# Mixture-of-experts stages on one core: per-tile combination weights from a row in device memory, spread over partitions by DMA, instead of from a selector matmul

## The chip, the core and the metric

The kernel runs on one core of a Trainium2 chip. The metric is the device time of one execution in microseconds, the median of several runs. TensorE (PE) does matmuls into PSUM, VectorE (DVE) and ScalarE (ACT) do elementwise work, GpSimd (POOL) does elementwise work on SBUF alone, SyncE (SP) issues DMAs.

## What is computed

The program is a chain of eight stages on N = 2048 tokens of 128 channels with a layer norm after each. Three of them are mixtures of experts; the change touches only these. For all tokens x, each with a sparse vector of weights `comb` over the experts:

```
m0:  8 experts, top 2:    out = sum_e comb[t,e] * ( gelu(x @ w1[e]) @ w2[e] )
m1: 64 experts, top 6:    out = shared(x) + sum_e comb[t,e] * ( (silu(x @ eg[e].T) * (x @ eu[e].T)) @ ed[e].T )
m2: 160 experts, top 8:   out = shared(x) + sum_e comb[t,e] * ( silu(x @ wg[e].T) @ wd[e].T )
```

Each stage also adds its input. Every expert is computed for every token, and `comb` is zero for those not chosen. A shared expert is one more with the weight 1.

## The kernel before

Activations lie transposed: 128 channels on the partitions, 2048 tokens along them, cut into NQ = 4 quarters of QW = 512. Hidden rows are worked on in units of 128 (one expert of m1 and m2 has 64, so a unit holds two of them; one expert of m0 has 256 and makes two units). m0 has 16 units, m1 33 and m2 81. One unit on one quarter is a tile, so the stages have 64, 132 and 324 tiles, 520 in all.

`Router` scores the experts, chooses and weighs them (`scores`, `weights`, in two halves of the tokens), and scales the chosen weights on ACT (L560). To keep float32 accuracy with bf16 matmuls it then cuts `comb` into three bf16 parts (L563, L565 on ACT, `rest` L651 on DVE), which PE turns (L530) and ACT and DVE copy out into `combT` (L569, L670). `combT` has 126 rows: three parts of a group of GE = 42 experts.

`experts_phase` is one block of five hand-ordered instruction streams, tied by counting semaphores. For tile k of unit s:

- PE: `product` makes the gate sums in three matmuls (fp16 high and low parts, L760); in m1 three more for the up sums; then the selector matmul (L786) multiplies a 126x128 matrix of zeros and ones by `combT` and so puts into a PSUM bank `cb` the 128x512 weights of this tile; then `down` of tile k-3 (three matmuls, L766) adds to the output sums.
- ACT: `h(k) = func(gate sums)` (L809), then `high(k-1)`, the fp16 high part of `hw` (L802).
- DVE: in m1 `hu(k) = h * up sums` (L841); `hw(k) = h (or hu) * cb` (L847); then `low(k-1) = hw - high` as fp16 (L829). Before `hw(k)` (in m1 before `hu(k)`) it waits for `lo_done` of `low(k-2)`, the instruction it issued last, whose input buffer `hw(k)` writes over.
- POOL: per unit, `split` of the next weights in `stage` into fp16 high (L745) and low (L747) parts, when the last `down` that used the slot is done. SP loads `stage` (L726), 128 KB a unit (192 KB in m1).

The banks 0 to 3 hold the output sums, the banks 4 to 7 alternate between gate, up and `cb`. Before gate(k), PE waits for `hw(k-2)`. The loops (`Fori`) have UB units in a body: 4 in m0, 3 in m1 and m2. The selector is reused with every 21 units, so m1 runs two loops one after the other and m2 four (of 7, 7, 7 and 6 bodies); m0 runs one of 4. ACT reloads its activation table (ACT_TABLE_LOAD) at the head of each body of a loop that was entered with another table; a loop that is entered with the right one has no load in it.

## Time and profile before

| | before |
|---|---|
| median of 3 runs | 2400.64 us (2400.48 to 2401.36) |
| profiled execution: its own time | 2406.57 us |
| its span, first to last instruction | 2404.8 us |
| busy: PE / DVE / ACT / POOL | 1962.0 / 1820.5 / 1370.3 / 254.4 us |
| mean granted clock of TensorE | 0.873 of 2.4 GHz |
| m0 / m1 / m2, from first gate to last gate matmul | from 306.8 / 638.2 / 1136.6 us on; the last gate matmul of all starts at 1629.8 us |

The profile was taken in one execution; line numbers are those of the kernel before. A matmul's length in it holds its pipelining (0.38 us for 128x512, while one starts every 0.216 us), so a rate of PE is read from starts or from counts in a window. The idle time of a group has the engine or DMA that ended it behind it.

### The profile page before, as it was taken

Reading aid. Unit: us, or ns where it says so; the run is one execution under the profiler, and the core shown is the slowest. Engines: PE = TensorE matmul, PEld = TensorE weight load, DVE = VectorE, ACT = ScalarE, POOL = GpSimd, SP = SyncE. Lnnn points to the kernel's source line nnn. Section 1 sums busy time; section 2 is a strip of 40 time slices with the busy share of each in tenths; the row PEclk is TensorE's granted clock in tenths of the full one; section 3 lists DMA queues with packets and bytes.
Section 4 is the critical chain, followed back from the end, with each engine's and each line's share of the span. In section 5 each row is a group of like instructions: output and inputs, shape, how many; then the busy total and the mean of one; then the engine's idle time right before and its main releaser. Section 6 shows DMA issues by size and latency. Waiting matters only on the chain. (4 is left out here: it accounts for less than half of the span.)

```text
span 2404.8 us, 49561 instructions
## 1 busy us (share of the span) xinstructions
PE 1962.0 (82%) x17365; PEld 1230.6 (51%) x17365; DVE 1820.5 (76%) x4154; ACT 1370.3 (57%) x3474; POOL 254.4 (11%) x321
## 2 busy tenths in 40 slices
PE   6999798576699996674999999996777676774987
PEld 5999644454344443453444444444455354443775
DVE  4444578787699996786888888887777877886776
ACT  5666477234455554644777777775455554553555
POOL 1000111000122221000222222220000000000000
PEclk9999899788699998896999999997878787785785
DMA  2000000100100000000000000000000000000000
GB/s 72 4 4 4 26 18 2 37 1 0 36 23 23 23 16 14 1 1 25 22 20 22 22 22 22 22 15 15 13 0 13 13 0 13 13 0 28 2 1 18
DMA packets 32343, 37.82 MB, mean 16 GB/s; under 512 B 4858, under 2 KB 30074, under 8 KB 31956
## 3 DMA queue, kind: packets, MB, share of 16 engines
q1 hardware_dynamic: 32212, 36.04, 5.1%
q8 instruction: 87, 1.43, 0.2%
q14 instruction: 44, 0.36, 0.0%
HBM read 33.40 MB, written 1.05 MB: 14 GB/s over the span
## 5 line engine op out<-in xcount | busy, mean ns | idle before, releaser
L809 ACT ACTIVATE m_h<-ps 128x512 f32<-128x512 f32 x520 | 310.4, 597 | 281.1 <-PE ps L760 280.9
L829 DVE TENSOR_TENSOR m_hwlo<-m_hw,m_hwhi 128x512 f16<-128x512 f32 x523 | 365.7, 699 | 0.3
L847 DVE TENSOR_TENSOR m_hw<-m_h,ps 128x512 f32<-128x512 f32 x388 | 267.0, 688 | 93.1 <-ACT m_h L809 81.1
L802 ACT ACTIVATE m_hwhi<-m_hw 128x512 f16<-128x512 f32 x523 | 325.4, 622 | 1.5 <-DVE m_hw L847 1.5
L760 PE MATMUL ps<-x_hi,m_whi 128*128 128x512 f16 x652 | 248.6, 381 | 4.6 <-issue 4.4
L760 PE MATMUL ps<-x_lo,m_whi 128*128 128x512 f16 x652 | 248.8, 382 | 0.0
L760 PE MATMUL ps<-x_hi,m_wlo 128*128 128x512 f16 x652 | 248.8, 382 | 0.0
L766 PE MATMUL ps<-m_hwhi,m_whi 128*128 128x512 f16 x529 | 201.6, 381 | 1.7 <-DVE m_hwlo L829 1.7
L766 PE MATMUL ps<-m_hwhi,m_wlo 128*128 128x512 f16 x529 | 200.6, 379 | 0.0
L766 PE MATMUL ps<-m_hwlo,m_whi 128*128 128x512 f16 x529 | 200.3, 379 | 0.0
L786 PE MATMUL ps<-m_combT,m_sel 126*128 126x512 bf16 x520 | 199.3, 383 | 0.0
L459 DVE TENSOR_TENSOR rn_s_lo<-rn_s_full,rn_s_hi 128x32 f16<-128x32 f32 x512 | 98.8, 193 | 131.1 <-ACT rn_s_full L416 131.1
L361 PE MATMUL ps<-rn_s_hi,rn_weights 128*128 128x8 f16 x4080 | 186.7, 169 | 0.0
L95 PE MATMUL ps<-ident,ln_x 128*128 128x128 f32 x320 | 75.0, 424 | 96.3 <-DVE ln_x L123 96.3
L414 ACT ACTIVATE rn_s_hi<-ps 128x32 f16<-128x32 f32 x512 | 100.9, 197 | 87.4 <-PE ps L378 47.4
L361 PEld LDWEIGHTS ps<-rn_s_hi,rn_weights 128*128 128x128 f16 x4080 | 149.1, 105 | 0.0
L378 PE MATMUL ps<-rn_s_lo,rn_weights 128*128 128x8 f16 x2040 | 141.1, 175 | 0.0
L747 POOL TENSOR_TENSOR m_wlo<-m_stage,m_whi 128x256 f16<-128x256 f32 (+1 forms) x130 | 134.9, 1038 | 10.4
L745 POOL CAST m_whi<-m_stage 128x256 f16<-128x256 f32 (+1 forms) x130 | 55.2, 425 | 722.1 <-PE ps L766 713.2
L95 PEld LDWEIGHTS ps<-ident,ln_x 128*128 128x128 f32 x320 | 63.3, 222 | 106.1 <-DVE ln_x L123 105.2
L841 DVE TENSOR_TENSOR m_hu<-m_h,ps 128x512 f32<-128x512 f32 x132 | 90.8, 688 | 24.9 <-PE ps L760 15.4
L760 PEld LDWEIGHTS ps<-x_hi,m_whi 128*128 128x128 f16 x652 | 63.0, 97 | 87.8 <-DVE m_hw L847 8.0
(435 smaller groups left out, 4614.5 us busy)
## 6 DMA issues: line engine op xcount, KB each, us to landing
m_stage<-in_m_w SPq DMA_DIRECT2D x97, 128.0 KB, 2.0
m_stage<-in_m_w SPq DMA_DIRECT2D x33, 192.0 KB, 2.3
lj_w<-in_lj_w SPq DMA_DIRECT2D x6, 768.0 KB, 4.3
lq_w<-in_lq_w SPq DMA_DIRECT2D x1, 1536.0 KB, 6.1
m_sel<-in_c_sel_pairs SPq DMA_DIRECT2D x2, 661.5 KB
la_w<-in_la_w SPq DMA_DIRECT2D x1, 1280.0 KB, 5.4
rn_rows<-in_L_attn_rows SPq DMA_DIRECT2D x4, 256.0 KB, 4.3
rn_xs<-rn_xn_hi SPq DMA_DIRECT2D x32, 32.0 KB, 1.9
```

The source lines that it names most:

```text
L95: last = nc.tensor.transpose(ps[:, G + g, j * P:(j + 1) * P], rows[:, 4 * g + j, :], ident[:])
L361: nc.tensor.matmul(sums[:, c, :], wt[:, n, :], s_hi[:, prev, n * B:(n + 1) * B], start=False, stop=False, skip_group_check=True)
L378: last = nc.tensor.matmul(sums[:, c, :], at_hi[:, n, :], s_lo[:, prev, n * B:(n + 1) * B], start=False, stop=(c == GP - 1), skip_group_che ...
L414: nc.scalar.activation(s_hi[:, t % (2 * K), g * W:(g + 1) * W], slot(g, t), ACT.Tanh)\
L747: nc.gpsimd.tensor_tensor(w_lo[:, s, :], stage[:, s, :], w_hi[:, s, :], ALU.subtract)\
L760: last = nc.tensor.matmul(out, a[:, s, cols], b[:, cut], start=(a is w_hi and b is x_hi), stop=(a is w_lo))
L766: last = nc.tensor.matmul(acc[n], a[:, s, COLS - P:COLS], b[:, k4, :], start=False, stop=False, skip_group_check=True)
L786: nc.tensor.matmul(cb, sel[0:3 * GE, bass.ds(j * UB + s, 1), :].rearrange("p u m -> p (u m)"), combT[0:3 * GE, g, n * QW:(n + 1) * QW], st ...
L802: nc.scalar.activation(hw_hi[:, k % 4, :], hw[:, k % 2, :], ACT.Copy).then_inc(hi_done, 1)
L809: nc.scalar.activation(h[:, k % 2, :], ps[:, 4 + (3 * k % 4 if gated else k % 2), :], func)\
L829: nc.vector.tensor_tensor(hw_lo[:, k % 4, :], hw[:, k % 2, :], hw_hi[:, k % 4, :], ALU.subtract)\
L847: nc.vector.tensor_tensor(hw[:, k % 2, :], src[:, k % 2, :], cb, ALU.mult).then_inc(hw_done, 1)
```

## The change

The selector matrices, `combT` in bf16 parts, and the cutting into parts are gone, and with them GE, the groups and the split of m1's and m2's loops: each stage is one loop now (4, 11 and 27 bodies).

The router turns the float32 weights directly (four transposes of 128x128 to a PSUM bank: a "turn" of 512 tokens and up to 128 experts; 4 turns in m0 and m1, 8 in m2), DVE and ACT copy out every other one, and ACT issues for each a DMA that stores it in a device-memory tensor with one row of 2048 float32 for each expert (m0_shares, m1_shares, m2_shares; 8, 66 and 162 rows).

In the expert loop, SP loads after the weights of a unit, and once all rows are stored, two DMAs into `comb`, a float32 tile of 128 x UB x 2048: each reads one row of 8 KB 64 times and writes it to 64 partitions, 512 KB each. They wait until the `hw` of the unit UB before is done. DVE waits once a unit for both and then takes the second operand of `hw` from SBUF. The selector matmul and its PSUM banks are gone, so the gate sums of m0 and m2 have four banks: PE may run gate(k) when `h(k-4)` is done (m1: `h(k-2)`), no longer after `hw(k-2)`. POOL's loop is the same but for the merged loops.

```diff
-        self.NG = NG = combT.shape[1]
-        self.EX = NG * GE
+        self.chunks = [slice(c, min(c + P, EX)) for c in range(0, EX, P)]
+        self.turns = [(h, c, q) for h in range(2) for c in range(len(self.chunks)) for q in range(2)]
...
-        self.comb, self.parts = sb("comb", [P, NT, self.EX]), sb("parts", [P, NT, NG, 3, GE], BF16)
+        self.comb, self.combT = sb("comb", [P, NT, EX]), sb("combT", [P, len(self.chunks), N])
...
+    def turned(self, n):
+        h, c, q = self.turns[n]
+        rows = self.chunks[c].stop - self.chunks[c].start
+        at = (2 * h + q) * QW
+        return self.combT[0:rows, c, at:at + QW], self.S.psum[0:rows, 4 + n % 4, :], self.rows[self.chunks[c], at:at + QW]
...
+        for n, (h, c, q) in enumerate(self.turns):
+            cols = self.chunks[c]
+            pe.wait_ge(self.scaled, h + 1)
+            if n >= 4:
+                pe.wait_ge(self.comb_out[n % 2], (n - 4) // 2 + 1)
+            for j in range(4):
+                last = nc.tensor.transpose(ps[0:cols.stop - cols.start, 4 + n % 4, j * P:(j + 1) * P],
+                                           self.comb[:, 8 * h + 4 * q + j, cols], self.S.ident[:])
+            last.then_inc(self.comb_up, 1)
         for engine in range(2):
-            pe.wait_ge(self.comb_out[engine], self.NG)
+            pe.wait_ge(self.comb_out[engine], len(self.turns) // 2)
...
-            act.wait_ge(self.scaled, h + 1)
-            nc.scalar.activation(self.parts[:, halves[h], :, 0, :], self.comb_v(h), ACT.Copy).then_inc(self.part0, 1)
-            act.wait_ge(self.rest1, h + 1)
-            nc.scalar.activation(self.parts[:, halves[h], :, 1, :], self.comb_v(h), ACT.Copy).then_inc(self.part1, 1)
-        for n in range(1, 2 * self.NG, 2):
-            act.wait_ge(self.comb_up, n + 1)
-            half, g = n // self.NG, n % self.NG
-            nc.scalar.activation(self.combT[0:3 * GE, g, half * 1024:(half + 1) * 1024],
-                                 ps[:, 4 + n % 4, :].bitcast(BF16)[0:3 * GE, :], ACT.Copy).then_inc(self.comb_out[1], 1)
+        for n in range(len(self.turns)):
+            out, turned, rows = self.turned(n)
+            if n % 2:
+                act.wait_ge(self.comb_up, n + 1)
+                nc.scalar.activation(out, turned, ACT.Copy).then_inc(self.comb_out[1], 1)
+            act.wait_ge(self.comb_out[n % 2], n // 2 + 1)
+            act.dma_start(rows, out).then_inc(self.stored, 16)
...
-        def rest(h, part):
-
-            dve.wait_ge(self.part0 if part == 0 else self.part1, h + 1)
-            out = self.comb_v(h) if part == 0 else self.parts[:, self.halves[h], :, 2, :]
-            nc.vector.tensor_tensor(out, self.comb_v(h), self.parts[:, self.halves[h], :, part, :], ALU.subtract)\
-                .then_inc(self.rest1 if part == 0 else self.part2, 1)
...
-        rest(0, 0)
-        rest(0, 1)
-        rest(1, 0)
-        turned(0, self.NG)
-        rest(1, 1)
-        turned(self.NG, 2 * self.NG)
-
-
-def experts_phase(nc, S, ctx, tag, weights, selector, combT, func, gated, UB, route):
+        for n in range(0, len(self.turns), 2):
+            out, turned, _ = self.turned(n)
+            dve.wait_ge(self.comb_up, n + 1)
+            nc.vector.tensor_copy(out, turned).then_inc(self.comb_out[0], 1)
...
+    assert bodies * UB == U
+    AHEAD = 2 if gated else 4
     LAG = 3
...
+    comb_got = [S.sems.new(f"{tag}_comb_got{s}") for s in range(UB)]
...
-    sel = sb("sel", [P, NSEL, P], BF16)
+    comb = sb("comb", [P, UB, N], F32)
...
+    def gate_bank(k):
+        return ps[:, 4 + (2 * (k % 2) if gated else k % 4), :]
+
+    def up_bank(k):
+        return ps[:, 5 + 2 * (k % 2), :]
...
-            sp.dma_start(sel[0:3 * GE], selector).then_inc(sel_got, 16)
-            for u0, bodies, _ in runs:
-                with sp.Fori(0, bodies) as j:
-                    for s in range(UB):
-                        sp.wait_ge(split_done, j * UB + (u0 + s + 1))
-                        sp.dma_start(stage[:, s, :], weights[bass.ds(j * UB + (u0 + s), 1)]
-                                     .rearrange("u p c -> p (u c)")).then_inc(slot_got[s], 16)
+            with sp.Fori(0, bodies) as j:
+                for s in range(UB):
+                    sp.wait_ge(split_done, j * UB + (s + 1))
+                    sp.dma_start(stage[:, s, :], weights[bass.ds(j * UB + s, 1)]
+                                 .rearrange("u p c -> p (u c)")).then_inc(slot_got[s], 16)
+                    if s == 0:
+                        sp.wait_ge(route.stored, 16 * len(route.turns))
+                    sp.wait_ge(hw_done, j * (4 * UB) + (4 * s + 4))
+                    for half in range(2):
+                        row = bass.ds(2 * (j * UB + s) + half, 1) if halves else bass.ds(j * (UB // 2) + s // 2, 1)
+                        sp.dma_start(comb[half * 64:half * 64 + 64, s, :], route.rows[row].broadcast_to([64, N]))\
+                            .then_inc(comb_got[s], 16)
...
-            for u0, bodies, g in runs:
-                with pe.Fori(0, bodies) as j:
-                    for s in range(UB):
-                        pe.wait_ge(split_done, j * UB + (u0 + s + 1 + UB))
-                        for n in range(NQ):
-                            k = 4 * s + n
-                            kk = j * (4 * UB) + (4 * u0 + k)
-                            R = 3 * k if gated else None
-                            hb = ps[:, 4 + (R % 4 if gated else k % 2), :]
-                            cb = ps[:, 4 + ((R + 2) % 4 if gated else 2 + k % 2), :]
-                            pe.wait_ge(hw_done, kk + 1)
-                            product(hb, slice(0, P), s, n).then_inc(gate_done, 1)
-                            if gated:
-                                pe.wait_ge(act_done, kk + 1)
-                                product(ps[:, 4 + (R + 1) % 4, :], slice(P, 2 * P), s, n).then_inc(up_done, 1)
-                                pe.wait_ge(hu_done, kk + 1)
-                            nc.tensor.matmul(cb, sel[0:3 * GE, bass.ds(j * UB + s, 1), :].rearrange("p u m -> p (u m)"),
-                                             combT[0:3 * GE, g, n * QW:(n + 1) * QW], start=True, stop=True)\
-                                .then_inc(comb_done, 1)
-                            pe.wait_ge(lo_done, kk + 1)
-                            down((s if n >= LAG else s - 1) % UB, (n - LAG) % NQ, (k - LAG) % 4)
+            with pe.Fori(0, bodies) as j:
+                for s in range(UB):
+                    pe.wait_ge(split_done, j * UB + (s + 1 + UB))
+                    for n in range(NQ):
+                        k = 4 * s + n
+                        kk = j * (4 * UB) + k
+                        pe.wait_ge(act_done, kk + (5 - AHEAD))
+                        product(gate_bank(k), slice(0, P), s, n).then_inc(gate_done, 1)
+                        if gated:
+                            pe.wait_ge(hu_done, kk + 1)
+                            product(up_bank(k), slice(P, 2 * P), s, n).then_inc(up_done, 1)
+                        pe.wait_ge(lo_done, kk + 1)
+                        down((s if n >= LAG else s - 1) % UB, (n - LAG) % NQ, (k - LAG) % 4)
...
-            act.sem_inc(act_done, 1)
+            act.sem_inc(act_done, 4)
...
-            for u0, bodies, _ in runs:
-                with act.Fori(0, bodies) as j:
-                    for k in range(4 * UB):
-                        kk = j * (4 * UB) + (4 * u0 + k)
-                        act.wait_ge(gate_done, kk + 1)
-                        nc.scalar.activation(h[:, k % 2, :], ps[:, 4 + (3 * k % 4 if gated else k % 2), :], func)\
-                            .then_inc(act_done, 1)
-                        act.wait_ge(hw_done, kk + 2)
-                        high(k - 1)
-            act.wait_ge(hw_done, 4 * U + 2)
+            with act.Fori(0, bodies) as j:
+                for k in range(4 * UB):
+                    kk = j * (4 * UB) + k
+                    act.wait_ge(gate_done, kk + 1)
+                    nc.scalar.activation(h[:, k % 2, :], gate_bank(k), func).then_inc(act_done, 1)
+                    act.wait_ge(hw_done, kk + 4 * UB)
+                    high(k - 1)
...
-            dve.sem_inc(hw_done, 2)
+            dve.sem_inc(hw_done, 4 * UB)
             dve.sem_inc(lo_done, LAG - 1)
             if gated:
-                dve.sem_inc(hu_done, 1)
+                dve.sem_inc(hu_done, 2)
...
+            with dve.Fori(0, bodies) as j:
+                for s in range(UB):
+                    for n in range(NQ):
+                        k = 4 * s + n
+                        kk = j * (4 * UB) + k
                         src = h
-                        dve.wait_ge(act_done, kk + 2)
+                        dve.wait_ge(act_done, kk + 5)
                         dve.wait_ge(lo_done, kk + 2)
                         if gated:
                             dve.wait_ge(up_done, kk + 1)
-                            nc.vector.tensor_tensor(hu[:, k % 2, :], h[:, k % 2, :], ps[:, 4 + (3 * k + 1) % 4, :],
-                                                    ALU.mult).then_inc(hu_done, 1)
+                            nc.vector.tensor_tensor(hu[:, k % 2, :], h[:, k % 2, :], up_bank(k), ALU.mult).then_inc(hu_done, 1)
                             src = hu
-                            dve.wait_ge(hu_done, kk + 2)
-                        dve.wait_ge(comb_done, kk + 1)
-                        cb = ps[:, 4 + ((3 * k + 2) % 4 if gated else 2 + k % 2), :]
-                        nc.vector.tensor_tensor(hw[:, k % 2, :], src[:, k % 2, :], cb, ALU.mult).then_inc(hw_done, 1)
+                            dve.wait_ge(hu_done, kk + 3)
+                        if n == 0:
+                            dve.wait_ge(comb_got[s], j * 32 + 32)
+                        nc.vector.tensor_tensor(hw[:, k % 2, :], src[:, k % 2, :], comb[:, s, n * QW:(n + 1) * QW], ALU.mult)\
+                            .then_inc(hw_done, 1)
                         dve.wait_ge(hi_done, kk + 1)
                         low(k - 1)
...
-    moe(nc, S, "m0", 8, A["m0_w"], A["c_sel_halves"], ACT.Gelu, False, 4,
+    moe(nc, S, "m0", 8, A["m0_w"], A["m0_shares"], False, ACT.Gelu, False, 4,
```

## Rows read from the trace of the kernel before

**Rows 1.** Groups by line of the page: busy, mean ns, idle before and releaser

```profile
L786 PE MATMUL ps<-m_combT,m_sel 126*128 126x512 bf16 x520 | 199.3, 383 | 0.0
```

**Rows 2.** Windows, one body each, last ten bodies: busy (instructions) by engine, PEclk, DMA

```profile
358.31:382.76 24.45, 24.42 (x114) 10.81 (x113) 21.00 (x33) 19.05 (x33) 5.40 (x8) 1.00 0.04 11
...
769.97:795.92 25.95, 25.95 (x122) 11.68 (x121) 23.76 (x37) 14.66 (x25) 5.41 (x7) 1.00 0.08 23
...
1249.34:1267.70 18.36, 18.33 (x86) 8.05 (x85) 15.77 (x25) 14.57 (x25) 4.00 (x6) 1.00 0.08 21
1267.70:1449.40 181.70, 181.70 (x841) 81.60 (x840) 156.73 (x241) 133.75 (x241) 41.76 (x60) 1.00 0.07 22
```

**Rows 3.** Timeline around a loop boundary in m2: start us, length, engine, line

```profile
1175.16 0.62 ACT L802 ACTIVATE m_hwhi<-m_hw 128x512 f16<-128x512 f32 x1
1175.30 0.69 DVE L847 TENSOR_TENSOR m_hw<-m_h,ps 128x512 f32<-128x512 f32 x1 [0.17 <-ACT m_h L809]
1175.80 1.28 ACT L809 ACT_TABLE_LOAD   x1
...
1177.10 0.60 ACT L809 ACTIVATE m_h<-ps 128x512 f32<-128x512 f32 x1
...
1177.82 0.69 DVE L847 TENSOR_TENSOR m_hw<-m_h,ps 128x512 f32<-128x512 f32 x1 [1.23 <-ACT m_h L809]
...
1178.42 0.68 DVE L829 TENSOR_TENSOR m_hwlo<-m_hw,m_hwhi 128x512 f16<-128x512 f32 x1
...
1179.19 0.69 DVE L847 TENSOR_TENSOR m_hw<-m_h,ps 128x512 f32<-128x512 f32 x1
...
1180.92 0.67 POOL L747 TENSOR_TENSOR m_wlo<-m_stage,m_whi 128x256 f16<-128x256 f32 x1
...
1181.18 0.96 DVE L829 TENSOR_TENSOR m_hwlo<-m_hw,m_hwhi 128x512 f16<-128x512 f32 x1
```

**Rows 4.** Timeline of another split of weights in m2

```profile
1149.80 0.40 POOL L745 CAST m_whi<-m_stage 128x256 f16<-128x256 f32 x1 [4.65 <-PE ps L766]
...
1149.95 0.80 DVE L829 TENSOR_TENSOR m_hwlo<-m_hw,m_hwhi 128x512 f16<-128x512 f32 x1
...
1150.28 0.99 POOL L747 TENSOR_TENSOR m_wlo<-m_stage,m_whi 128x256 f16<-128x256 f32 x1
...
1150.86 0.69 DVE L847 TENSOR_TENSOR m_hw<-m_h,ps 128x512 f32<-128x512 f32 x1
```

**Rows 5.** Timeline of VectorE in m1

```profile
804.24 0.69 DVE L841 TENSOR_TENSOR m_hu<-m_h,ps 128x512 f32<-128x512 f32 x1
804.97 0.69 DVE L847 TENSOR_TENSOR m_hw<-m_hu,ps 128x512 f32<-128x512 f32 x1
...
806.35 0.69 DVE L841 TENSOR_TENSOR m_hu<-m_h,ps 128x512 f32<-128x512 f32 x1
```

**Rows 6.** ACT groups by line and form: ACT table loads

```profile
L809 ACT ACT_TABLE_LOAD x18 | 23.1, 1283 | 0.3
```

**Rows 7.** Window in the stage before m2: busy by engine, granted clock (1.00)

```profile
1000.00:1020.00 20.00, 17.59 (x203) 12.94 (x201) 18.56 (x45) 11.01 (x23) 0.00 (x0) 1.00 0.01 2
```

**Rows 8.** Timeline at the end of m2's router

```profile
1120.02 0.20 DVE L645 RECIPROCAL m2r_rec<-m2r_sum 128x8 f32<-128x8 f32 x1
...
1122.91 2.64 ACT L560 ACTIVATE m2r_comb<-m2r_comb,m2r_rec 128x160 f32<-128x160 f32 x8
...
1138.85 0.69 DVE L847 TENSOR_TENSOR m_hw<-m_h,ps 128x512 f32<-128x512 f32 x1 [3.80 <-ACT m_h L809]
```

**Rows 9.** Windows in which the DMA queues were full: last columns share, GB/s

```profile
8.00:10.00 2.00, 0.73 (x4) 0.33 (x2) 0.00 (x0) 1.98 (x12) 0.00 (x0) 1.00 1.02 268
2185.00:2186.00 1.00, 0.00 (x0) 0.00 (x0) 0.00 (x0) 0.00 (x0) 0.00 (x0) 0.50 1.13 467
```

**Rows 10.** DMA issues of the page: KB each, us to landing

```profile
m_stage<-in_m_w SPq DMA_DIRECT2D x97, 128.0 KB, 2.0
```

**Rows 11.** SP's timeline: length of one DMA issue

```profile
2181.41 0.43 SPq L1856 DMA_DIRECT2D lq_w<-in_lq_w  x1
```

More of the change, by code:

```diff
@@ L663, in vector, with experts_phase @@
         weights(1)
-        def turned(first, last):
-            for n in range(first, last):
-                if n % 2 == 0:
-                    dve.wait_ge(self.comb_up, n + 1)
-                    half, g = n // self.NG, n % self.NG
-                    nc.vector.tensor_copy(self.combT[0:3 * GE, g, half * 1024:(half + 1) * 1024],
-                                          ps[:, 4 + n % 4, :].bitcast(BF16)[0:3 * GE, :]).then_inc(self.comb_out[0], 1)
-        rest(0, 0)
-        rest(0, 1)
-        rest(1, 0)
-        turned(0, self.NG)
-        rest(1, 1)
-        turned(self.NG, 2 * self.NG)
-def experts_phase(nc, S, ctx, tag, weights, selector, combT, func, gated, UB, route):
+        for n in range(0, len(self.turns), 2):
+            out, turned, _ = self.turned(n)
+            dve.wait_ge(self.comb_up, n + 1)
+            nc.vector.tensor_copy(out, turned).then_inc(self.comb_out[0], 1)
+def experts_phase(nc, S, ctx, tag, weights, halves, func, gated, UB, route):
     U, _, COLS = weights.shape
-    NSEL = selector.shape[1]
+    bodies = U // UB
+    assert bodies * UB == U
+    AHEAD = 2 if gated else 4
     LAG = 3
@@ L689, in experts_phase @@
     acc = [ps[:, n, :] for n in range(NQ)]
[L690 to L692 removed]
+    zeroed = S.sems.new(f"{tag}_zeroed")
+    gate_done, up_done, act_done, hu_done, hw_done, hi_done, lo_done, down_done, split_hi, split_done, \
+        split_start = S.sems.new(*(f"{tag}_{n}" for n in ("gate", "up", "act", "hu", "hw", "hi", "lo", "down",
                                                           "split_hi", "split", "split_start")))
     slot_got = [S.sems.new(f"{tag}_slot{s}") for s in range(UB)]
+    comb_got = [S.sems.new(f"{tag}_comb_got{s}") for s in range(UB)]
     x_hi, x_lo = S.x_hi, S.x_lo
@@ L709, in open_sums @@
                              skip_group_check=True)
-    runs = []
-    for g in range((U + NSEL - 1) // NSEL):
-        runs.append((g * NSEL, (min(U, (g + 1) * NSEL) - g * NSEL) // UB, g))
-    assert sum(r[1] for r in runs) * UB == U
+    def gate_bank(k):
+        return ps[:, 4 + (2 * (k % 2) if gated else k % 4), :]
+    def up_bank(k):
+        return ps[:, 5 + 2 * (k % 2), :]
     with nc.Block(no_gpsimd_drain=True) as block:
@@ L830, in low @@
                     .then_inc(lo_done, 1)
-            for u0, bodies, _ in runs:
-                with dve.Fori(0, bodies) as j:
-                    for k in range(4 * UB):
-                        kk = j * (4 * UB) + (4 * u0 + k)
+            with dve.Fori(0, bodies) as j:
+                for s in range(UB):
+                    for n in range(NQ):
+                        k = 4 * s + n
+                        kk = j * (4 * UB) + k
                         src = h
-                        dve.wait_ge(act_done, kk + 2)
+                        dve.wait_ge(act_done, kk + 5)
                         dve.wait_ge(lo_done, kk + 2)
@@ L2227 @@
         A[name] = nc.dram_tensor(f"in_{name}", a.shape, mybir.dt.from_np(a.dtype), kind="ExternalInput").ap()
+    for name, rows in (("m0_shares", 8), ("m1_shares", 66), ("m2_shares", 162)):
+        A[name] = nc.dram_tensor(name, (rows, N), F32).ap()
     out = nc.dram_tensor("out", (B, T, C), F32, kind="ExternalOutput").ap()
```

71 lines of the change are left out of this document (22 added, 49 removed).

## Prediction, made before the changed kernel was run

> **What bounds the kernel now.** I read the groups by line first. The selector matmul is a group of 520 with 0.0 us of idle before it [rows 1]: PE runs it back to back with its neighbours, so it costs PE time wherever PE sets the pace. Then the windows, one loop body each, tell where that is. Ten bodies of m2 take 181.70 us and hold 841 matmuls, which is 120 tiles of 7 [rows 2]: 0.216 us a matmul, 1.514 us a tile, PE never idle, granted clock 1.00. Likewise m1: 122 records, 12 tiles of 10 matmuls, 25.95 us, 2.163 us a tile. So all three stages are bound by PE, and a tile would be 6 x 0.216 = 1.30 us of PE (m0, m2) or 9 x 0.216 = 1.95 us (m1) without the selector.
>
> The next limit is DVE, and busy shares hide how near it is. In m2 its two instructions follow each other at 0.60 us (hw to low, 1177.82 to 1178.42), and at 0.77 us (low to the next hw, 1178.42 to 1179.19) [rows 3]: the second step is the whole length of `low`, 0.68, and 0.09 until the semaphore lets `hw` go, since `hw(k)` waits for the `low` just issued. That wait is in the changed code too. A tile can't be under 0.60 + 0.77 = 1.37 us on DVE. In m1, `hu` to `hu` is 2.11 us with no idle between [rows 5]; its floor is 2.11, just 0.05 below PE's 2.163.
>
> **The change, part by part.**
>
> *Selector matmul removed.* It takes 0.216 us of PE from each of 520 tiles, 112 us in all. But the pace goes over to DVE at once: the floor falls from 1.514 to 1.37 (not 1.30) in m0 and m2, and from 2.163 to 2.11 (not 1.95) in m1. For a body: m2 12 x 1.37 = 16.44 us, m0 16 x 1.37 = 21.92, m1 12 x 2.11 = 25.32. The gate banks, now four, keep PE ahead: its wait is for a `down` behind `low`, and from there to the `hw` four tiles on, there is room. ACT does two instructions of 0.60 and 0.62 a tile and isn't near 1.37. PE will have gaps of some 0.1 to 0.2 us a tile. A stage with PE at 17.59 of 20 us kept the clock at 1.00 [rows 7], so I give the clock nothing.
>
> *`hw` reads its weights from SBUF, not PSUM.* This is the term that decides. POOL splits each unit's weights in two instructions, and in the trace these and `low`, which reads two SBUF tiles, shut each other out. `low`, issued 0.15 us after the cast at 1149.80, takes 0.80 instead of 0.68, so the cast held it until 0.27 after its start; the subtraction issued at 1150.28 takes 0.99 instead of its 0.67 alone, so it began at 1150.60, which is 0.53 after `low` really began (1150.07) [rows 3, 4]. And `low` issued 0.26 after a subtraction that ran at once takes 0.96, so that one held for 0.54 [rows 3]. `hw` with one input in PSUM is not touched: 0.69 in the middle of a subtraction [rows 4]. After the change `hw` has the operands of `low`, so I count it as `low`. In m2 the split is released by a `down` that follows `low(j)`: 0.68 for `low`, 0.05, two matmul starts 0.43, and some 0.60 to POOL makes 1.76 us after the start of `low(j)`. `low(j+1)` then reads (1.37 to 1.90), the cast gets in from 1.90 to 2.17, and `hw(j+3)`, due at 2.14, is 0.03 late. The subtraction asks at about 2.38, when `hw(j+3)` reads until 2.70, and holds until 3.24; `low(j+2)`, due 0.60 after `hw`, at 2.77, is 0.47 late. Sum c = 0.50 us a unit. If DVE kept its turn from `hw` to `low` (due only 0.07 us after `hw` lets go), the subtraction would slip in after `low` and delay `hw` by 0.30: c = 0.33. I take 0.50, since the release at 0.53 comes before the next issue at 0.60. The ends are 0 and 0.50 + 0.20. In m1 the same walk lets the cast in behind `hw` and delays `low` by 0.33, and puts the subtraction beside `hu`, which has a PSUM input: c = 0.33, ends 0 and 0.80.
>
> The Trainium skill (SBUF — State Buffer, "Who interferes with whom") says the same of any VectorE instruction with two SBUF inputs against a GpSimd one that reads SBUF: whoever issues first keeps the port for its whole instruction. It speaks for counting `hw` like `low`; no row here shows an `hw` of this form.
>
> *One loop for each stage.* ACT loads its table 18 times at L809 [rows 6]: 4 in m0, 7 in m1's first loop, 7 in m2's first, none in the later loops. With single loops these are 4, 11 and 27. Before, a load costs m2's body 18.36 - 18.17 = 0.19 us [rows 2]. Paced by DVE it costs more: from `high` (1175.16) over the load and `h` to `hw` (1177.82) is 2.66 us [rows 3], `high` starts 0.69 + 0.03 after its `hw`, so from one `hw` to the second after it is 3.38 against 2 x 1.37 = 2.74: 0.64 us a body. Ends 0.19 and 0.70. In m1 the same path ends at 3.3 against 3.5 for DVE, so the load stays hidden.
>
> *The bodies.* m2: 16.44 + 3 x 0.50 + 0.64 = 18.58, times 27 = 501.7; before 7 x 18.36 + 20 x 18.17 = 491.9 [rows 2]: **+9.8 us**. m0: 21.92 + 4 x 0.50 + 0.64 = 24.56 against 24.45, four bodies: +0.4. m1: 25.32 + 3 x 0.33 = 26.31 against 25.95, eleven bodies: +4.0.
>
> *Router.* Gone: two conversions on ACT and two subtractions on DVE for each half, and bf16 transposes. New: float32 transposes, copies, stores, a wait for the stores, and 1 MB that must land before the first `hw`. In m2, weighing of half two ends on DVE at 1120.2; the scaling takes 2.64 us [rows 8], to 1122.9. ACT then has 4 copies of 0.60 and 8 issues of 0.43 [rows 11], which makes 5.8, to 1128.7, the last store 2.0 us to land [rows 10], two issues 0.9, 2 us fixed and 1.05 MB at 268 GB/s [rows 9] 3.9 us: 1137.5, against 1138.85 for the first `hw` before [rows 8]. So -1.3 for m2; with fewer removed steps about +2 in m0 and 0 in m1. Together +0.3; ends -8 and +12 by the rate of the DMAs. ACT's issues have the whole loop's `h` behind them, but that waits for this data anyway.
>
> *1 MB a unit by DMA.* Per unit 1.05 MB and 0.13 MB of weights. m2's unit is 18.58 / 3 = 6.2 us, so 190 GB/s are enough to hide it; the queues ran at 268 and 467 GB/s in full windows, with rows of 4 KB and 12 KB to 128 partitions [rows 9]. SP's three issues, 1.3 us a unit [rows 11], fit. Behind SP's new wait for the `hw` of unit u-3 stands the weights' load of the next unit, used more than a unit later, and the rows for unit u have two units of time. I take it as hidden. No row shows a DMA to 64 partitions of this size or one that reads the same 8 KB 64 times; the nearest rows give 2.5 to 4.4 us a unit, and if half the partitions gave half the rate, 5.1 to 8.8.
>
> The Trainium skill speaks against this part (SBUF — State Buffer, "Door 1: The DMA port swizzle"): partitions 0 to 63 reach 8 of 16 ports, 196 GB/s measured for 1 MiB and about 218 at best, and two DMAs to the two halves go one after the other. By it the rows would take 4.8 to 5.4 us and the weights 0.3, an estimate from that page: 5.1 to 5.7 us a unit, hidden under my 6.2, but not under m2's floor without POOL, 5.7.
>
> *Sum:* +9.8 + 0.4 + 4.0 + 0.3 = +14.5 us. The profiled execution took 2406.57 us (span 2404.8), so it would show 2421.1; the runs' median lies 5.9 below it, and the same sum on it is 2400.6 + 14.5 = **2415**. This case reaches from 2396 (c = 0.33 in m2 and m0, a load at 0.4) to 2430.
>
> **The rivals.**
>
> *B: the new `hw` doesn't collide with POOL, or little (faster).* For it: only `low` was seen to. Against: same operands. With c = 0: m2's body 17.08, 27 x 17.08 = 461.2, -30.7; m0 22.56, -7.6; m1 25.32, -6.9; the start +0.3: 2355.7. With half the collisions about 2385.
>
> *C: the row DMAs set the pace (far slower).* One mechanism: two half-width transfers in a row, all from one 8 KB row. It decides from 1.18 MB / 6.2 us = 190 GB/s downwards; it makes m2 slower than before from 1.18 / 6.06 = 195. For it: half of 268 is 134. Against: half of 467 is 233. At 170 GB/s a unit of m0 and m2 takes 6.94 us, (6.94 - 6.07) x 97 units = +84: about 2490 with the slower starts; at 134, 8.8 us and 2690. Its sign would be DVE waiting for `comb` at the first tile of each unit.
>
> *D: PE stays the bound* (1.30 us a tile, 324 x 0.214 = 69 us gained in m2 alone). I exclude it: `low` and its semaphore alone stand against it, unless `low` to `hw` gets shorter.
>
> **How the numbers follow.** Forecast 0.58, B 0.24, C 0.18. Range: leaving out B's lowest tenth and C below 175 GB/s or so leaves 2356 to 2470. What a measurement here can tell from no change is about 0.2%, 4.8 us. Faster: B and 0.03 of the forecast's low end, 0.27. Same: 0.11 of the forecast and 0.01 of C, 0.12. Slower: 0.44 and 0.17, 0.61.
>
> **What would show it.** In m2 after: `low` to `hw` at 0.77 and tiles at 1.37 away from splits; `hw` or `low` of 1.0 to 1.2 us beside each POOL subtraction; bodies near 18.6 (m0 24.6, m1 26.3); 27 table loads with a DVE idle of 0.6 behind each; no idle of DVE that a DMA of `comb` ends, but for the first of each stage. It is wrong if `hw` keeps 0.69 beside POOL (B), if `comb` ends idle time at each unit (C), or if the clock falls below 1.00 in the loops.

## The result and the profile after

The kernel after takes 2414.11 us, the median of 12 runs (2404.91 to 2419.51), beside 2401.02 for the kernel before in 12 runs (2397.67 to 2404.4): ratio 1.0052, 95% interval 1.004 to 1.0064, so 9.6 to 15.4 us slower. The forecast was 2415, which is 14.5 us above the kernel before. The profiled execution took 2408.58 us (span 2406.8).

That one lies only 2 us above the profiled execution of before, which would mislead. The start of the layer norm ahead of m0 and that of the one behind m2 tell more. View: ACT's timeline, first before, then after (start us, length, engine, line):

```profile
271.19 0.30 ACT L151 ACTIVATE ln_sd<-ln_mv,epsilons 128x8 f32<-128x8 f32 x1 [1.82 <-DVE ln_mv L110]
...
1639.80 0.30 ACT L151 ACTIVATE ln_sd<-ln_mv,epsilons 128x8 f32<-128x8 f32 x1 [2.34 <-DVE ln_mv L110]
...
1911.16 0.30 ACT L151 ACTIVATE ln_sd<-ln_mv,epsilons 128x8 f32<-128x8 f32 x1 [7.83 <-DVE ln_mv L110]
1955.81 0.30 ACT L151 ACTIVATE ln_sd<-ln_mv,epsilons 128x8 f32<-128x8 f32 x1 [1.82 <-DVE ln_mv L110]
```

```profile
270.24 0.30 ACT L151 ACTIVATE ln_sd<-ln_mv,epsilons 128x8 f32<-128x8 f32 x1 [1.82 <-DVE ln_mv L110]
...
1648.50 0.30 ACT L151 ACTIVATE ln_sd<-ln_mv,epsilons 128x8 f32<-128x8 f32 x1 [1.82 <-DVE ln_mv L110]
...
1919.56 0.30 ACT L151 ACTIVATE ln_sd<-ln_mv,epsilons 128x8 f32<-128x8 f32 x1 [7.65 <-DVE ln_mv L110]
1960.83 0.30 ACT L151 ACTIVATE ln_sd<-ln_mv,epsilons 128x8 f32<-128x8 f32 x1 [1.82 <-DVE ln_mv L110]
```

From first to second it is 1368.61 us before and 1378.26 after: the three expert stages and the unchanged layers between them cost **9.65 us** more. Behind m2 the code is the same, yet one layer there took 44.65 us before (1911.16 to 1955.81) and 41.27 after. Such steps of some 3 us fall differently in other profiled executions too (from the layer norm behind m2 to the end it is 754 to 765 us in all the traces, whatever the edit); they can hide a difference of this size in one pair of executions.

The groups by line and form, and the DMA issues, of after:

```profile
L806 DVE TENSOR_TENSOR m_hwlo<-m_hw,m_hwhi 128x512 f16<-128x512 f32 x523 | 409.7, 783 | 0.3
L824 DVE TENSOR_TENSOR m_hw<-m_h,m_comb 128x512 f32<-128x512 f32 x388 | 273.5, 705 | 69.1 <-DMA m_comb<-m_shares 25.0 <-ACT m_h L787 12.5
L753 PE MATMUL ps<-m_hwhi,m_whi 128*128 128x512 f16 x529 | 208.6, 394 | 72.6 <-DVE m_hwlo L806 66.8
L787 ACT ACT_TABLE_LOAD x42 | 53.9, 1283 | 2.4 <-ACT m1r_combT L564 0.6 <-ACT m0r_combT L564 0.6 <-ACT m2r_combT L564 0.5
...
m_comb<-m_shares SPq DMA_DIRECT2D x260, 512.0 KB, 6.3
m_stage<-in_m_w SPq DMA_DIRECT2D x97, 128.0 KB, 5.9
```

The selector group [rows 1] is gone, and PE now waits for DVE: 66.8 us before `down`, ended by `low` (L753). `low` was 0.699 on the mean before and is 0.783; table loads went from 18 [rows 6] to 42; the weights land 5.9 us behind their issue, 2.0 before [rows 10]. The 25.0 us that the row DMAs end are 10.4 in m0 and 14.6 in m2, each at the first `hw` of its stage. The `hw` of m1 form a group of their own, with 5.7 us at the first.

Windows of one body in m1 and in m2, and of three bodies, of after (length; busy PE, PEld, DVE, ACT, POOL with instructions; granted clock, DMA share, GB/s):

```profile
723.88:750.22 26.34, 25.32 (x110) 9.59 (x109) 24.71 (x36) 14.68 (x25) 6.03 (x6) 1.00 0.61 142
...
1202.60:1220.93 18.33, 16.96 (x74) 6.06 (x73) 17.04 (x24) 15.61 (x26) 4.58 (x6) 1.00 0.86 193
...
1300.00:1355.00 55.00, 50.90 (x218) 18.15 (x216) 51.11 (x73) 46.84 (x76) 13.76 (x18) 1.00 0.87 194
```

m2's body takes 18.33 us with 12 matmuls fewer, against 18.17 and 18.36 [rows 2]. PE, whose rows filled 181.70 of 181.70 us there, has gaps now. The timelines of ACT, DVE and POOL at the head of such a body show what keeps DVE from its 1.37 us a tile. The first line is the `low` beside the last split of the body before:

```profile
1309.74 1.15 DVE L806 TENSOR_TENSOR m_hwlo<-m_hw,m_hwhi 128x512 f16<-128x512 f32 x1
...
1310.49 1.28 ACT L787 ACT_TABLE_LOAD   x1
...
1310.99 0.69 DVE L824 TENSOR_TENSOR m_hw<-m_h,m_comb 128x512 f32<-128x512 f32 x1
...
1312.60 0.69 DVE L824 TENSOR_TENSOR m_hw<-m_h,m_comb 128x512 f32<-128x512 f32 x1 [0.31 <-ACT m_h L787]
1313.21 0.68 DVE L806 TENSOR_TENSOR m_hwlo<-m_hw,m_hwhi 128x512 f16<-128x512 f32 x1
1313.93 0.69 DVE L824 TENSOR_TENSOR m_hw<-m_h,m_comb 128x512 f32<-128x512 f32 x1
1314.54 0.69 DVE L806 TENSOR_TENSOR m_hwlo<-m_hw,m_hwhi 128x512 f16<-128x512 f32 x1
...
1314.97 0.51 POOL L733 CAST m_whi<-m_stage 128x256 f16<-128x256 f32 x1 [4.63 <-PE ps L753]
1315.56 0.99 POOL L735 TENSOR_TENSOR m_wlo<-m_stage,m_whi 128x256 f16<-128x256 f32 x1
...
1315.26 0.77 DVE L824 TENSOR_TENSOR m_hw<-m_h,m_comb 128x512 f32<-128x512 f32 x1
1315.95 1.16 DVE L806 TENSOR_TENSOR m_hwlo<-m_hw,m_hwhi 128x512 f16<-128x512 f32 x1
1317.21 0.69 DVE L824 TENSOR_TENSOR m_hw<-m_h,m_comb 128x512 f32<-128x512 f32 x1
```

Away from splits the pace is near what was foreseen: `low` to `hw` is 0.72 here (1313.21 to 1313.93) and 0.79 most often in m2, `hw` to `low` 0.61 (1313.93 to 1314.54), so a tile takes 1.33 to 1.40. `hw` beside the cast takes 0.77, `low` beside the subtraction 1.16. All over m2, 77 `low` take 1.15 or 1.16 us: about one a unit.

### The profile page after: what moved, and what is told of

It reads as the page before. It is cut to its first block and busy times, and to the rows that moved or that the text cites. A ratio compares the mean times of both kernels' runs of the same rounds, so it can differ in the third digit from the quotient of the medians.

```text
span 2406.8 us, 49587 instructions
## 1 busy us (share of the span) xinstructions
PE 1910.8 (79%) x16797; PEld 1135.3 (47%) x16797; DVE 1859.8 (77%) x4142; ACT 1419.0 (59%) x3487; POOL 277.9 (12%) x321
## 3 DMA queue, kind: packets, MB, share of 16 engines
q8 instruction: 83, 1.36, 0.2%
## 5 line engine op out<-in xcount | busy, mean ns | idle before, releaser
L806 DVE TENSOR_TENSOR m_hwlo<-m_hw,m_hwhi 128x512 f16<-128x512 f32 x523 | 409.7, 783 | 0.3
L824 DVE TENSOR_TENSOR m_hw<-m_h,m_comb 128x512 f32<-128x512 f32 x388 | 273.5, 705 | 69.1 <-DMA m_comb<-m_shares 25.0
L753 PE MATMUL ps<-m_hwhi,m_whi 128*128 128x512 f16 x529 | 208.6, 394 | 72.6 <-DVE m_hwlo L806 66.8
L753 PE MATMUL ps<-m_hwlo,m_whi 128*128 128x512 f16 x529 | 202.8, 383 | 0.0
L753 PE MATMUL ps<-m_hwhi,m_wlo 128*128 128x512 f16 x529 | 202.5, 383 | 0.0
L753 PEld LDWEIGHTS ps<-m_hwhi,m_whi 128*128 128x128 f16 x529 | 51.1, 97 | 305.2 <-DVE m_hwlo L806 302.0
L733 POOL CAST m_whi<-m_stage 128x256 f16<-128x256 f32 (+1 forms) x130 | 77.9, 599 | 708.0 <-PE ps L753 548.1
L735 POOL TENSOR_TENSOR m_wlo<-m_stage,m_whi 128x256 f16<-128x256 f32 (+1 forms) x130 | 135.5, 1042 | 10.4
L747 PEld LDWEIGHTS ps<-x_hi,m_whi 128*128 128x128 f16 x652 | 64.2, 99 | 89.1 <-issue 10.4
L1954 ACT ACTIVATE lq_e<-ps,lq_neg 128x256 f32<-128x256 f32 x128 | 59.6, 470 | 77.9 <-DVE lq_neg L2017 58.6
```

Source lines behind the costliest of these rows:

```text
L735: nc.gpsimd.tensor_tensor(w_lo[:, s, :], stage[:, s, :], w_hi[:, s, :], ALU.subtract)\
L747: last = nc.tensor.matmul(out, a[:, s, cols], b[:, cut], start=(a is w_hi and b is x_hi), stop=(a is w_lo))
L753: last = nc.tensor.matmul(acc[n], a[:, s, COLS - P:COLS], b[:, k4, :], start=False, stop=False, skip_group_check=True)
L806: nc.vector.tensor_tensor(hw_lo[:, k % 4, :], hw[:, k % 2, :], hw_hi[:, k % 4, :], ALU.subtract)\
L824: nc.vector.tensor_tensor(hw[:, k % 2, :], src[:, k % 2, :], comb[:, s, n * QW:(n + 1) * QW], ALU.mult)\
```

## The experiments

All edits are to the kernel after, but for two that are to the kernel before. A time without a number of runs beside it is that of one execution. The diffs show the lines that matter, and `...` stands for the rest.

**POOL's splits of later bodies taken out.**

```diff
-            with pool.Fori(0, bodies) as j:
-                ... split of unit j * UB + s
+            for s in range(UB):
+                ... split of unit s
+            with pool.Fori(0, bodies - 1) as j:
+                ... the same waits, and pool.sem_inc(split_done, 1), for each unit
```

> The kernel after, but POOL splits the weights of the first body of each expert stage only; every later unit uses the split weights of the first body again (they are loaded as before, not used), so the output is another. SP's loads, the row transfers, and all work of PE, ACT and DVE stay. Theory (DVE sets the pace, and each low of about 1.15 us, where 0.68 is the rule, is POOL's subtraction beside it): no low or hw above 0.8 us, m2's unit falls from 6.1 to about 5.6, its body from 18.33 to about 17.1, m1's low from 0.99 to 0.69 and its body from 26.35 to some 25.5 to 26.0, the whole about 2414 - 27 x 1.2 - 11 x 0.5 - 4 = 2372 us. Rival (the row transfers, at 193 GB/s over the unit, are near the most that the queue gives, and set the pace): the units of m2 stay at 6.0 to 6.1, and DVE's idle before hw, ended by the row transfer, takes the place of the longer low: about 2405 or more.

2368.73 us, and behind the first body of each stage no `low` or `hw` is over 0.70. m2's body 17.30 us, its units 5.44, 5.58 and, over the body's end, 6.28; m1's body 25.43. The transfers then ran at 205 GB/s, so at 193 they were not at their limit. Groups and window of DVE, 1250 to 1450 us and 1300 to 1355 us:

```profile
L828 DVE TENSOR_TENSOR m_hw<-m_h,m_comb 128x512 f32<-128x512 f32 x139 | 96.2, 692 | 20.7 <-ACT m_h L791 9.4
L810 DVE TENSOR_TENSOR m_hwlo<-m_hw,m_hwhi 128x512 f16<-128x512 f32 x139 | 95.2, 685 | 0.0
...
1300.00:1355.00 55.00, 53.17 (x231) 19.27 (x230) 49.49 (x78) 49.30 (x81) 0.00 (x0) 1.00 0.95 204
```

So POOL costs m1's unit (26.34 - 25.43) / 3 = 0.30 us and m2's body 1.03, and the rival that the DMAs pace falls. What was not expected is that ACT's `h` now ends 22.6 us of DVE's idle in m2, where it is 9.9 us with all splits. Behind each table load but the first it is 0.79 us here and 0.31 with all splits. The waits of DVE in m2, and the first `hw` behind a load:

```profile
DVE m_hw L828 <- ACT m_h L791: 22.6, 29, 1.3
DVE m_hw L828 <- DMA m_comb<-m_shares: 14.3, 1, 14.3
...
1308.59 0.69 DVE L828 TENSOR_TENSOR m_hw<-m_h,m_comb 128x512 f32<-128x512 f32 x1 [0.79 <-ACT m_h L791]
```

**The table brought in ahead of the loop.**

```diff
             route.scalar(act)
+            nc.scalar.activation(primed[:], S.one, func)
```

> The kernel after with one more activation of one column with the stage's own function on ACT, behind the router and ahead of the loop, so that the loop is entered with the right table and needs no load at the head of each body. The result is unchanged. Theory by the prediction: a load costs m2's and m0's bodies 0.64 us (31 bodies), m1's nothing: 2414 - 20 = 2394 us, m2's body 17.7. Rival by the trace of after, in which ACT ends only about 0.3 us of DVE's idle at each head of a body: 2414 - 31 x 0.3 = 2405 us, m2's body 18.0. If the load is hidden altogether: 2414, m2's body 18.3. Table loads of these stages: 42 before the edit, 3 with it.

2409.03 us (10 runs), 1.0022 of before (1.0007 to 1.0036). m2's body is 18.15: a load costs 0.18 us, not 0.64, and ACT ends less than 1 us of the idle before `hw` in the whole of m2. From first to last `hw` m2 takes 488.45 us, 5.46 less than after. m1 is unchanged at 26.35. This and the run before it belong together: at the head of a body ACT falls behind by about 0.8 us. With all splits, the `low` just ahead of it (1309.74 in the kernel after) is held to 1.15 by the last split of the body before, so that DVE itself comes late and waits only 0.31. Delays of two engines at about one place hide each other, so they can't be added. With the load away, POOL's share is (18.15 - 16.44) / 3 = 0.57 us a unit. The 16.44 is the floor of 12 x 1.37 of the prediction; a kernel with two buffers and neither load nor later splits was not run.

**The rows by DMA only once.**

```diff
+            (ahead of the loop: the weights and rows of the first UB units, as before)
-            with sp.Fori(0, bodies) as j:
+            with sp.Fori(0, bodies - 1) as j:
...
-                    for half in range(2):
+                    for half in range(0):
...
-                            dve.wait_ge(comb_got[s], j * 32 + 32)
+                            dve.wait_ge(comb_got[s], 32)
```

> The kernel after, but the rows of the combination weights are brought in by DMA for the first body of each stage only; later bodies multiply by the same rows again, so the output is another. The loads of the weights and all work of the engines stay. Theory (the row transfers are hidden and cost nothing but their start at each stage): m2's and m1's bodies 18.3 and 26.3 as with the transfers, landing of the weights 2.0 to 2.3 us in place of 5.9, total within 3 us of the kernel after. Rival (they set the pace, or take SBUF from the engines): bodies of m2 fall to 17.5 or less, by 20 us and more in all.

2405.91 us, 8 below the median of the kernel after and inside the spread of its runs. m2's body 18.30, m1's 26.24, m0 96.38 us from first to last `hw` in place of 96.71, and the weights land in 2.0 us again (rows below). 126 MB less of traffic are worth 27 x 0.03 + 11 x 0.1 + 0.3, some 2 us in all by the loops: hidden, as the prediction had it.

```profile
m_stage<-in_m_w SPq DMA_DIRECT2D x97, 128.0 KB, 2.0
m_comb<-m_shares SPq DMA_DIRECT2D x20, 512.0 KB, 10.5
```

**One transfer to 128 partitions.**

```diff
-                    for half in range(2):
-                        row = ... 2 * (j * UB + s) + half ...
-                        sp.dma_start(comb[half * 64:half * 64 + 64, s, :], route.rows[row].broadcast_to([64, N]))
+                    row = ... 2 * (j * UB + s) ...
+                    sp.dma_start(comb[:, s, :], route.rows[row].broadcast_to([P, N]))
```

> The kernel after with one row transfer for a unit, one row to all 128 partitions (1 MB in one DMA in place of two of 512 KB each to 64 partitions), so in m1 and m2 the second expert of a pair has the weights of the first, and the output is another. If the two halves share the DMA engines already, the 1 MB takes what the two took: the last byte 6 to 7.8 us behind the issue, weights still 5.9 behind the issue. If each half is limited by the 64 partitions that it writes, the one DMA lands its 1 MB in about 4 to 5 us, and the first hw of m2 comes 1 to 3 us earlier. Bodies of all stages as in after, 18.3 and 26.35, by both.

2405.56 us. The 1 MB lands in 4.8 us, where each 512 KB took 6.3 behind its own issue; first `hw` of m2 at 1139.87 (after: 1146.12, its stage began 3.2 us later). For the same bytes the engines' share in 1250 to 1450 us is 0.53 against 0.87. Bodies stay at 18.33 and 26.35.

```profile
m_comb<-m_shares SPq DMA_DIRECT2D x130, 1024.0 KB, 4.8
```

**Two transfers, each over all partitions.**

```diff
-                        sp.dma_start(comb[half * 64:half * 64 + 64, s, :], ...)
+                        sp.dma_start(comb[half::2, s, :], ...)
...  (and the hidden rows of a pair of experts interleaved in the weights)
```

> The kernel after, but each of the two row transfers writes every other partition over all 128 in place of 64 neighbours, and the two experts of a pair stand on even and odd hidden partitions (the weights are laid out so on the host). The result is unchanged. One transfer to 128 partitions landed 1 MB in 4.8 us where the two of 64 take 6.4; if it is the reach over all partitions that counts, the two striped ones land in about 5 us, the weights in 4.5, and the first hw of m2 comes 5 us earlier, those of m0 and m1 2 us: -8 us at the most, 2406 us. If it is the count of DMAs or packets, the landing stays at 6.4 and the time at 2414. Bodies 18.3 and 26.35 in both.

2404.97 us (10 runs), 1.0002 of before (0.999 to 1.0015); the landing falls to 4.4 us (weights 4.1), bodies 18.33 and 26.35, first `hw` of m0 and m2 at 309.76 and 1140.31. It is thus the neighbourhood of the 64 partitions, not the count of DMAs. The gain is 12 us by the two ratios (1.0052 and 1.0002), where 8 at the most were expected. In the trace it is 6 as far as the end of m2, and these come from the stages' starts; the rest of the 12 is not accounted for.

**Four buffers `hw`.**

```diff
-    hw = sb("hw", [P, 2, QW], F32)
+    hw = sb("hw", [P, 4, QW], F32)      # and hw[:, k % 4, :] in hw, high and low
...
-                        dve.wait_ge(lo_done, kk + 2)
+                        dve.wait_ge(lo_done, kk + 1)
```

> The kernel after with four buffers hw in place of two, so that hw(k) no longer waits for the low(k-1) issued just ahead of it, but for low(k-2). The result is unchanged. Theory (the 0.77 us from low to hw, where hw to low takes 0.60, is this wait, and DVE paces): DVE then takes 2 x 0.60 = 1.20 us a tile and PE is the bound again with 6 matmuls of 0.216 = 1.30 us; unit 5.2 to 5.3, m2's body 15.7 to 16.2 in place of 18.33, m1's (3 DVE operations 1.80, PE 9 x 0.216 = 1.95) 23.4 to 24.5 in place of 26.35, m0's 21 to 21.6 in place of 24.9; together -57 - 25 - 13 = about 2320 us. Rival (each unit needs 1.18 MB by DMA, and the most seen so far is 205 GB/s): the transfers become the bound in m2 and m0, unit 5.8, body 17.3, about 2350 us. Second rival (low's own length of 0.68 is DVE's time and the wait costs nothing): bodies as in after, 2414 us.

2358.61 us (4 runs), 0.9818 of before (0.9795 to 0.9842), where 2320 was expected. m2's body 17.19, m1's 24.47. The wait was what the theory said: `hw` starts 0.60 behind `low` now. But PE did not become the bound in m2: a body still pays for POOL, which meets a busier DVE, and for the table load, so that it is 1.0 us above the upper end expected. The transfers' rival came near in its number (body 17.3, 2350 us), yet not by its mechanism, for in m2 a row DMA ends idle time of DVE only at the first `hw`.

**Both, four buffers and the table primed.**

> Four buffers hw and the activation ahead of the loop that brings the table in. The result is unchanged. In the kernel after the load cost 0.18 us a body (18.33 against 18.15), in the one without later splits it stood at the head of each body with 0.8 us. With PE as the bound and only 1.28 us of ACT behind 1.30 us tiles, the load should cost 0.2 to 0.7 us a body: 6 to 22 us less than with the buffers alone. If the transfers are the bound, the load is hidden and nothing is gained.

2330.94 us (4 runs), 0.97 of before (0.9676 to 0.9723). That is 28 us less than with the buffers alone, where 6 to 22 were expected. m2's body 16.47: the load costs 0.72 us here, 0.18 in the slower kernel. In m1, where it cost nothing with two buffers, it costs 0.33 (24.47 to 24.14). In 1300 to 1355 us DVE is busy for 55.00 of 55.00 us. Timeline of DVE and POOL:

```profile
1299.96 0.68 DVE L808 TENSOR_TENSOR m_hwlo<-m_hw,m_hwhi 128x512 f16<-128x512 f32 x1
1300.56 0.68 DVE L826 TENSOR_TENSOR m_hw<-m_h,m_comb 128x512 f32<-128x512 f32 x1
1301.16 0.88 DVE L808 TENSOR_TENSOR m_hwlo<-m_hw,m_hwhi 128x512 f16<-128x512 f32 x1
1301.97 1.15 DVE L826 TENSOR_TENSOR m_hw<-m_h,m_comb 128x512 f32<-128x512 f32 x1
1303.04 0.68 DVE L808 TENSOR_TENSOR m_hwlo<-m_hw,m_hwhi 128x512 f16<-128x512 f32 x1
...
1300.60 0.90 POOL L734 CAST m_whi<-m_stage 128x256 f16<-128x256 f32 x1 [2.92 <-PE ps L754]
1301.58 0.99 POOL L736 TENSOR_TENSOR m_wlo<-m_stage,m_whi 128x256 f16<-128x256 f32 x1
```

Here it is mostly the new `hw` that takes 1.15 beside the subtraction (57 times in m2, `low` 23 times); with a PSUM input it took 0.69 in that place [rows 4]. By the starts, the cast costs 0.21 (1301.16 to 1301.97 is 0.81) and the subtraction 0.47 (1301.97 to 1303.04 is 1.07), so the unit is 8 x 0.60 + 0.21 + 0.47 = 5.48 us; measured 5.49.

**The same without the later splits.**

> Four buffers hw, the table primed, and POOL splitting the weights of the first body of each stage only (later units use these again, so the output is another). With the splits the unit of m2 is 5.49. Theory (DVE paces it still: 4 x 1.20 and 0.69 of slowing beside POOL's subtraction): without POOL the unit falls to PE's 4 x 6 x 0.216 = 5.2, m1's body from 24.1 to 23.4 (12 x 1.95), total 2331 - 81 x 0.29 - 11 x 0.7 - 4 = 2295 to 2300 us. Rival (the transfers pace it: 1.18 MB at 215 GB/s is 5.49): the unit stays at 5.49, total 2320 or more.

2305.57 us, between what the two theories said, and each holds for a part. m1's body is 23.21, PE's pace. m2's second is 15.53, PE's pace too, and from the fifth body on is 15.94 to 15.98: the row DMAs now end 42.9 us of DVE's idle in m2, in 71 waits, where it was some 14 us and one wait before. Group (1250 to 1450 us), window and issues:

```profile
L830 DVE TENSOR_TENSOR m_hw<-m_h,m_comb 128x512 f32<-128x512 f32 x151 | 103.5, 685 | 15.9 <-DMA m_comb<-m_shares 15.9
...
1300.00:1355.00 55.00, 54.76 (x250) 23.42 (x249) 50.85 (x85) 46.97 (x84) 0.00 (x0) 1.00 1.03 221
...
m_comb<-m_shares SPq DMA_DIRECT2D x260, 512.0 KB, 9.0
```

This is the prediction's rival C at last, at 222 GB/s. It needed the wait for `low`, the table loads and the splits out of the way first.

**And with striped transfers.**

> Four buffers hw, the table primed, striped row transfers, and POOL splitting the weights of the first body of each stage only (later units use these again, so the output is another). Without the stripes this kernel had units of 5.21, 5.42, 5.33 in m2 (mean 5.32, 222 GB/s), and row transfers ended 42.9 us of DVE's idle there. Theory (two transfers of 64 partitions, one after the other, give no more than 222 GB/s): with the stripes the idle goes, the unit falls to PE's 24 x 0.216 = 5.18, m2's body from 15.97 to 15.55, and with the earlier starts the whole from 2306 to 2285 to 2293 us. Rival (a limit of another kind, of the queue or of reading the same row): units and landing stay, 2298 us or more.

2287.0 us, as the theory had it (2285 to 2293). m2's body is 15.54, m1's 23.21, m0's 20.72: 1.295, 1.934 and 1.295 us a tile, PE's pace in all three. The same views as above:

```profile
L830 DVE TENSOR_TENSOR m_hw<-m_h,m_comb 128x512 f32<-128x512 f32 x155 | 107.2, 692 | 2.6 <-DVE m_hwlo L812 2.4
...
1300.00:1355.00 55.00, 55.00 (x257) 24.89 (x256) 54.40 (x86) 47.33 (x85) 0.00 (x0) 1.00 0.65 228
...
m_comb<-m_shares SPq DMA_DIRECT2D x260, 512.0 KB, 4.4
```

More bytes a second at a share of 0.65 instead of 1.03.

**All that keeps the result:** four buffers, primed table, stripes.

> Four buffers hw, the table primed, and striped row transfers, all in one. The result is unchanged. With PE as the bound everywhere: m2's body 12 x 1.30 = 15.6 to 16, m1's 23.4 to 24, m0's 20.8 to 21.3; about 2300 to 2310 us. If the transfers were the bound in the two kernels without the stripes, this one is 20 us or more below them; if not, within 8 us.

2331.69 us (4 runs), 0.9701 of before (0.968 to 0.9721), no better by the median than without the stripes (2330.94), and some 20 us above what was expected with PE as the bound. m2's unit is 5.49 in both, so the DMAs did not pace it; DVE did, busy for 200.00 of 200.00 us from 1250 to 1450. In the trace m2 ends 5 us earlier than without stripes, and 4 of these are gone at the program's end in layers that the edit doesn't touch. Whether the stripes bring anything here stays open.

**Are these gains owed to the change?** The same edits to the kernel before: the primed table alone, then with four buffers.

> The kernel before with the activation that brings in the stage's table ahead of its loops. The result is unchanged. Its 18 loads at the head of a body cost 0.19 us each where the bodies with and without stand side by side (18.36 and 18.17): by that -18 x 0.19 = -3.4 us plus 3 x 1.3 us for the activation ahead, within 4 us of the kernel before. If the loads cost 0.64 each there too: -8 us.

> The kernel before with both edits that made the kernel after 84 us faster: four buffers hw and the primed table. The result is unchanged. Theory (PE paces the kernel before with 7 matmuls a tile, and DVE is ahead of it): the bodies stay at 18.1 and 25.9, the total within 8 us of the kernel before. Rival (DVE's wait costs the kernel before as well, its tile of 1.514 being no PE floor): it falls by 20 us or more, and the gain owes nothing to the rows.

2401.04 us, 0.9991 of before (0.998 to 1.0001), and 2401.03 us, 0.9994 (0.9982 to 1.0006). Bodies 18.18 in m2 and 25.95 in m1, in both. There PE paces with 7 matmuls a tile (10 in m1), and neither edit shows a gain beyond the noise; in the kernel after they are worth 3.5%.

## Why the prediction was right

| step | forecast, us | measured, us |
|---|---|---|
| m2's body | 18.58 | 18.33 |
| m1's body | 26.31 | 26.34 |
| m0's body | 24.56 | 24.79 and 25.04 (second and third) |
| POOL, a unit of m2 / m1 | 0.50 / 0.33 | 0.57 (table primed) / 0.30 |
| table load, a body of m2 | 0.64 | 0.18 |
| first `hw` against before, m0, m1, m2, from the layer norm ahead | +2, 0, -1.3 | +3.2, +0.8, +1.8 |
| first to last `hw`, m0, m1, m2 | +0.4, +4.0, +9.8 | -0.9, +3.4, +1.9 |
| all | +14.5 | +9.65 in the trace, +13.1 by the medians (9.6 to 15.4) |

*The pace goes over to DVE at 1.37 us a tile.* Right. Without POOL's later splits a tile of m2 takes 1.36 to 1.40. Four buffers take the wait for the `low` just issued away, and make it 1.20 where neither POOL nor a load intervenes. D was rightly excluded: PE's 1.30 was reached only with that wait, the table load and the splits gone.

*The new `hw` counts like `low`.* Right, and the size too, though the walk was off in detail. I had the cast make `hw` 0.03 late; it made it 0.08 late, and was itself held (0.51 in place of 0.40 [rows 4]). `low`'s 0.47 came as forecast. B, with 0.24, has fallen: `hw` doesn't keep 0.69 beside POOL, it takes 0.77 beside a cast in the kernel after, and 1.15 beside a subtraction with four buffers. But how much of POOL's 0.57 is owed to the new operand was not isolated. `low` read two SBUF tiles before the change too, and met POOL then (0.80 to 0.96 in 26 of its 325 instructions in m2) while DVE had time to spare. B's `c = 0` left that share out, and no kernel was run that is paced by DVE and reads the weights from PSUM. The Trainium skill (SBUF — State Buffer, "Who interferes with whom") says that a VectorE instruction with two SBUF inputs contends with a GpSimd one that reads SBUF; the trace agrees, 1.15 against 0.69. The section's wording that the first keeps the port for the whole instruction, which the prediction repeated, is more than the rows show: there `low` let the subtraction in 0.53 us after its own start, of 0.68.

*The table load at 0.64.* Wrong by a factor of 3.5, the largest mis-sized term: 27 x (0.64 - 0.18) = 12 us too much in m2. My path from `high` to the next `hw` started at a DVE that is never late itself. The sign named for it, 0.6 us of idle behind each load, did not come: it was 0.31. The kernel without later splits shows that a load leaves DVE 0.79 us idle when POOL does not delay it, and the one with the primed table that it costs a body 0.18 when POOL does. I had added two delays of which one covers the other.

*The starts.* Forecast +0.3, measured +5.8 together: too low by 5.5 us, inside the ends given (-8 and +12). 3.1 us of it are m2's. Timeline of ACT, SP and DVE at m2's start, after:

```profile
1124.99 0.20 DVE L641 RECIPROCAL m2r_rec<-m2r_sum 128x8 f32<-128x8 f32 x1
...
1125.88 2.00 ACT L558 ACTIVATE m2r_comb<-m2r_comb,m2r_rec 128x160 f32<-128x160 f32 x6
...
1133.49 0.26 ACTq L566 DMA_DIRECT2D m_shares<-m2r_combT  x1
...
1138.29 1.19 SPq L715 DMA_DIRECT2D m_comb<-m_shares  x2
...
1146.12 0.69 DVE L824 TENSOR_TENSOR m_hw<-m_h,m_comb 128x512 f32<-128x512 f32 x1 [14.64 <-DMA m_comb<-m_shares]
```

From the end of the scaling (1127.88) to that of the last store's issue (1133.75) it is 5.87 us, forecast 5.8. But SP then waited 4.54 for the stores, not the 2.0 in which a load of weights lands, and the first rows 7.83 from the start of their issue, not 6.8. The router itself saved time: its scaling began 33.9 us behind the start of the layer norm ahead (1125.23 and 1091.31), 37.1 us before the change (1122.91 [rows 8] and 1085.79).

*Rows hidden.* Right. In the loops no `hw` waits for a DMA, and taking the rows away gains 0.03 us a body in m2 and 0.10 in m1. The prediction had the DMAs decide from 190 GB/s a unit downwards, and they gave 193, 205 and 215 as the units got shorter, and 222 at most. So the margin was 0.8 us a unit (1.18 MB / 222 GB/s = 5.3 against 6.1), and the chance of 0.18 for C was not idle. The Trainium skill (SBUF — State Buffer, "Door 1: The DMA port swizzle") gives about 218 GB/s as the best for partitions 0 to 63, and has them on half of the ports. The trace agrees within 2%, though a ninth of its bytes are weights that go to all partitions, and the striped transfers agree with its cause.

*The sum.* It came out near by errors of opposite sign. Table loads were 12 us too high and POOL in m2 81 x 0.07 = 5.7 too low, the starts 5.5 too low; m1's loop was 0.6 too high and m0's 1.3. That makes 3 of the 4.85 us by which the forecast is above the trace; the rest is not assigned. The interval of the medians holds the forecast and, at its lower end, the 9.65 of the trace. What adds 3.5 us to the medians stays open. So the direction and the order of the terms were understood, but a hit within 1 us of 2415 is luck.
